# The order of weight mixing and residual rests on GpSimd in the third FFN step of a macaron block

## What is computed

```
w_eff = w * (su @ sv)                 # su, sv of rank 4
a = x @ gate_eff.T ; b = x @ up_eff.T # 512 -> 1792
d = silu(a) * b
out = d @ down_eff.T                  # 1792 -> 512
```

## Time and profile before

| | |
|---|---|
| median of 3 runs | 1234.85 us (1234.61 to 1234.9) |
| profiled execution, its own time | 1236.1 us |
| span of its instructions | 1234.8 us |
| busy: TensorE, VectorE, ScalarE, GpSimd | 1216.9, 828.5, 757.9, 652.9 us |
| mean granted TensorE clock | 0.999 |
| DMA traffic | 93.77 MB, mean 76 GB/s |

### The profile page before, as it was taken

One profiled execution on the slowest core, in us unless ns is written; L12 is line 12 of the kernel. 1 busy time (PEld: TensorE's weight loads), 2 busy tenths in 40 slices (PEclk: granted clock), 3 DMA queues, 4 the chain that ended last, 5 costly groups with the idle time before them and its releaser, 6 DMA issues.

```text
span 1234.8 us, 18595 instructions
## 1 busy us (share of the span) xinstructions
PE 1216.9 (99%) x6418; PEld 1068.0 (86%) x6418; DVE 828.5 (67%) x2002; ACT 757.9 (61%) x1762; POOL 652.9 (53%) x526
## 2 busy tenths in 40 slices
PE   6999999999999999999999999999999999999999
PEld 5888888899999999999999999999999788888887
DVE  7876665775666677677667667677677768745555
ACT  4554442357667677777767767767767764544442
POOL 4786551735675625725724724824823343865540
PEclk9999999999999999999999999999999999999999
DMA  6143232212213123122122122122122110221101
GB/s 232 43 154 110 102 104 102 95 44 86 85 36 103 45 76 103 44 78 100 38 86 95 43 86 94 44 86 87 51 86 78 26 54 16 70 68 52 52 18 68
DMA packets 33452, 93.77 MB, mean 76 GB/s; under 512 B 4112, under 2 KB 4784, under 8 KB 31312
## 3 DMA queue, kind: packets, MB, share of 16 engines
q1 hardware_dynamic: 33120, 92.29, 22.0%
q10 hardware_dynamic: 240, 0.30, 0.1%
HBM read 62.69 MB, written 29.88 MB: 75 GB/s over the span
## 4 chain that ended last, share of the span: by engine, by line
PE 92%; DVE 4%; ACT 2%; POOL 1%; issue 1%; DMA 1%; SPq 0%; DVEq 0%; ACTq 0%; POOLq 0%
PE bank L345 21%; PE bank L347 21%; PE bank L346 21%; PE bank L591 5%; PE bank L430 4%; PE bank L424 4%; PE bank L425 4%; PE bank L605 3%; PE bank L610 3%; PE bank L606 3%; PE bank L570 2%; PE bank L373 1%; DVE stats L1116 1%; PE bank L573 1%; PE bank L361 0%
## 5 line engine op out<-in xcount | busy, mean ns | idle before, releaser
L974 ACT ACTIVATE prob<-prob,neg_top 128x128 f32<-128x128 f32 (+3 forms) x256 | 141.2, 553 | 78.4 <-DVE neg_top L1386 77.8
L1665 POOL TENSOR_TENSOR rows<-rows,row_root_y 128x640 f32<-128x640 f32 x64 | 80.5, 1258 | 204.2 <-DVE row_root_y L1112 204.2
L1659 POOL TENSOR_TENSOR square<-rows 128x640 f32<-128x640 f32 x64 | 79.3, 1256 | 161.0 <-DVE rows L1422 125.1
L1534 POOL TENSOR_TENSOR w_l_late<-raw_late,w_h_late 128x512 fp32r<-128x512 f32 (+1 forms) x59 | 91.5, 1565 | 73.9 <-ACT w_h_late L728 73.9
L983 ACT ACTIVATE prob<-prob,inverse 128x128 f32<-128x128 f32 (+3 forms) x256 | 123.0, 553 | 4.4 <-DVE inverse L1391 4.4
L1397 DVE TENSOR_TENSOR probT_l<-bank,probT_h 128x512 fp32r<-128x512 f32 x160 | 101.4, 684 | 20.9 <-ACT probT_h L989 20.8
L1386 DVE CUSTOM_DVE_ANT_0 prob<-bank,bias 128x128 f32<-128x128 f32 (+3 forms) x256 | 110.0, 485 | 0.6 <-PE bank L347 0.4
L989 ACT CAST probT_h<-bank 128x512 fp32r<-128x512 f32 x160 | 84.6, 597 | 42.0 <-PE bank L591 42.0
L1178 DVE SCALAR_TENSOR_TENSOR x_rows<-bank,x_rows 128x512 f32<-128x512 f32 x112 | 75.7, 687 | 46.0 <-PE bank L430 45.9
L345 PE MATMUL bank<-o_h,oT_h 128*128 128x512 f32 x256 | 104.8, 409 | 0.0
L347 PE MATMUL bank<-o_h,oT_l 128*128 128x512 f32 x256 | 100.9, 394 | 0.0
(11 more groups left out here) (216 smaller groups left out, 3757.3 us busy)
## 6 DMA issues: line engine op xcount, KB each, us to landing
x_ring<-x_between SPq DMA_DIRECT2D x64, 256.0 KB, 2.6
x_between<-x_ring SPq DMA_DIRECT2D x56, 256.0 KB, 2.0
raw_late<-w_qkv SPq DMA_DIRECT2D x8, 1536.0 KB, 6.4
raw_early<-ffn_w SPq DMA_DIRECT2D x21, 512.0 KB, 4.1
scaled<-raw_early SPq DMA_DIRECT2D x21, 512.0 KB, 2.7
raw_late<-scaled SPq DMA_DIRECT2D x21, 512.0 KB, 3.7
raw_late<-w_o SPq DMA_DIRECT2D x8, 1024.0 KB, 5.0
x_between<-x_rows SPq DMA_DIRECT2D x8, 256.0 KB, 2.0
```

The source lines that it names most:

```text
L974: last = act.activation(p, p, ACT.Exp, bias=neg_top[:, h:h + 1], scale=-1.0, accum_out=total[:, h:h + 1])
L1534: return pool.tensor_tensor(lo, raw, hi.bitcast(F32), ALU.subtract)
```

## The change

In `ffn` GpSimd mixes the weights of step 2 before the rests of a11 and a12 of the same step, in both passes. Since the end of the mixing no longer says that the rest of a12 was made from the raw block, the load of "gu0" of step 3 waits for that rest as well, as the loads before it do.

```diff
                 if p == 0:
                     stack_ahead(2)
+
+                mix_weights(p, 2)
                 split(p, 2, "a11", "a12")
-                mix_weights(p, 2)
...
                 if kind == "gu0" and seven(p, s - 1):
                     sp.wait_ge(weights_mixed, 4 * sevens(p, s - 1))
-                if kind != "gu0" or s - 1 <= 1:
+                if kind != "gu0" or s - 1 <= 2:
                     sp.wait_ge(ffn_lo, split_nth(p, s - 1, {"gu0": "a12", "gu1": "a22", "down": "d1"}[kind]) + 1)
```

## The result

| | before | changed |
|---|---|---|
| median, six runs each | 1234.87 us (1234.61 to 1236.34) | 1246.71 us (1245.37 to 1247.05) |
| ratio, 95% interval | | 1.0088 (1.0077 to 1.0098) |
| profiled execution, its span | 1236.1, 1234.8 us | 1245.37, 1244.1 us |
| mean granted clock, profiled | 0.999 | 0.997 |

The change costs 11.8 us by the medians. The forecast was 1245.2, the range 1242.0 to 1248.0. First the page of the changed kernel, part 1; it answers to the earlier trace rows.

A forecast was written before the change was run, and what follows sets the result against it. TensorE was taken to bound the kernel, so GpSimd's lateness goes straight onto the end. 6.2 + 3.5 - 0.9 + 1.6 = 10.4 us on the median of 1234.85 gives 1245.2 us, range 1242.0 to 1248.0.

The forecast's parts named there:

- What bounds the kernel: Whole kernel: TensorE, busy 1216.9 us; other engines' lateness beyond product 1's slack in step 2 goes straight onto the end.
- Stall of pass 0, 6.2 us: TensorE at product 1 of step 2, pass 0: waits for a11's rest until 79.05, 6.2 us, bounds 4.9 to 6.8.
- the d_lo that I named at 77.35: VectorE operation in pass 0, 1.02 us, claimed not to move and to fall beside a11's rest, taken as 1.81 us.
- Stall of pass 1, 3.5 us: TensorE at product 1 of step 2, pass 1: 3.5 us, bounds 2.3 to 4.5, with mixing starting in GpSimd's 2.56 us wait.
- The stall of 0.87 us saved: TensorE's later stall at 91.19 in pass 0 goes as step 3's load gains slack: -0.9 us.
- The added wait: Step 3's first load, waiting for a12's rest: goes out 0.5 us earlier in pass 0; in pass 1 mends no stall, 0.
- The clock, 1.6 us: TensorE's clock falls to half after pass 0's stop, +1.6 us; nothing counted for pass 1 in the likeliest case.
- the row at 986: Clock fall near the end of attention in the earlier profile, 3.4 us long, 1.6 us lost; used to size the clock term.
- No fall: Rival: clock stays at 1.00 after TensorE's long stop in pass 0; 1243.7 us, chance 0.25.
- Delay made up in attention: Rival: the 3.4 us of idle time in attention shrinks and makes up some delay; 1241.8 us, chance 0.03.
- Not slower: Rival: mixing hides in GpSimd's wait for ScalarE's copy of a11, only 0.9 us saved; 1234.0 us, chance 0.02.
- Two falls, 1246.8: Rival: the clock falls after the stops of both passes, adding 1.6 us to 1245.2; chance 0.2.

The follow-up runs named there:

- pass 0 alone: Changed kernel with the mixing ahead of the rests in pass 0 only, pass 1 in the old order: 1241.89 us, ratio 1.0059.
- the filled kernel: Changed kernel plus overwritten matmuls in TensorE's stops ahead of product 1 of step 2, 24 in pass 0 and 13 in pass 1: 1243.77 us.
- the second profile: Changed kernel run once more with no edit: median 1247.31 us, ratio 1.0097; its profiled execution took 1247.88 us.

## Why the prediction was right, point by point

- **What bounds the kernel.** Right: TensorE's slack of under 0.3 us at product 1 in pass 0 and none in pass 1 was the whole matter. Moving the mixing behind a11's rest alone gave all the time back. Of what was put back and what was put ahead, TensorE in the kernel before asks for the rest of a11 at once, for that of a12 in product 2, at 81.47, and for the first mixed block in product 6:

```profile
84.22 0.39 PE L345 MATMUL bank<-mix_h,mixed_h 128*128 128x512 f32 x1
```

- **Stall of pass 0, 6.2 us.** Measured 6.03. The mixing took 5.85 for 5.96 and the rest of a11 1.68 for 1.81, and by the chain of work it ended at 78.96, for 79.0. But the d_lo that I named at 77.35 was not what it met. VectorE's timeline in the changed kernel:

```profile
71.87 3.06 DVE L1217 TENSOR_TENSOR d_lo<-d,d_hi 128x512 fp32r<-128x512 f32 x2
...
76.30 1.53 DVE L1211 TENSOR_TENSOR d<-d,silu 128x512 f32<-128x512 f32 x1 [0.17 <-ACT silu L772]
83.11 0.69 DVE L1217 TENSOR_TENSOR d_lo<-d,d_hi 128x512 fp32r<-128x512 f32 x1 [5.27 <-ACT d_hi L782]
```

  ScalarE's copy ahead of that d_lo stands behind product 1's partial sum, so it moved to 83.11, and I had said that it doesn't move. The pair of d_lo from 71.87 took 3.06 us, 1.98 before, and VectorE's product at 76.30 was the one beside the rest. The duration that I took was near, the reason given for it was not right.
- **Stall of pass 1, 3.5 us.** Measured 3.3. The mixing started right behind the down rests, as said. It was closer than I wrote. The chain that ended last, in the changed profile:

```profile
1067.82 3.58 DMA raw_late<-scaled
...
1071.55 1.28 POOL mixed L1562
...
1076.23 1.68 POOL mixed L1568
1077.90 1.23 POOL w_l_late L1534
```

  The load landed at 1071.40 and the mixing began 0.15 us later. The two durations were both off, and that they cancel is luck: the mixing took 6.4 us (1071.55 to 1077.91) for my 5.95, and the rest of a11 1.23 for my 1.75, together 7.6 for 7.7. The VectorE operation that I had meet the rest did meet it, at 1078.14, but there it was the one that took longer, 1.53 us for 0.69 at 1066.16 before.
- **The stall of 0.87 us saved.** Right in the changed kernel, 1.1 us with what hangs on it. Of the 6.7 us of slack that I gave the load, the part that counts is the late TensorE; the 0.5 us by the clock are not needed. SyncE's queue after:

```profile
80.25 7.02 SPq L1801 DMA_DIRECT2D raw_early<-ffn_w  x2
```

  Step 3's first load went out at 80.25 for 80.81. The kernel with the mixing between the rests, with its load at 80.87 and TensorE on time, kept the stall; the kernel with half of the mixing ahead, with its load at 80.94 and TensorE 3.4 us late, lost it.
- **The added wait.** Right, 0.
- **The clock, 1.6 us.** This is the term that was mis-sized. Pass 0's fall cost 2.5 us, because the half clock lasted from 77.3 to 84.1, 5.1 us of it with TensorE at work, and not for the 3.4 us of the row at 986. And there is a second fall, for which I counted nothing and gave a chance of 0.2: six of the ten runs of the changed kernel have a mean clock of 0.996, as the profile with two falls has. The one such profile has it behind pass 1's stop. In the kernel with pass 0 alone no run of four had 0.996, which speaks for that stop and against the old place near 987; more profiles would have to show it. With the measured terms 6.0 + 3.3 + 2.5 - 1.1 = 10.7 us, on the 1234.8 of the kernel before without a fall, comes 1245.5: two of the first six times lie there (1245.37, 1245.65). With 1.6 more for a second fall comes 1247.1, and the other four lie at 1246.5 to 1247.05, so the median is of that kind. Three of these four have the clock of 0.996; the slowest, 1247.05, has 0.997, as has the 1243.46 of pass 0 alone, so not every long run is explained by a second fall. The kernel before is without a fall in most runs (46 of 68 in four batches have a mean clock of 1.000). That the clock is nearly all of the remainder is shown by the filled kernel: 8.6 us without any fall, where the measured stalls give 8.2 and my terms without a fall 8.8. The forecast is 1.5 us under the median: too small by 0.9 in pass 0's fall and by the 1.6 of the second, too large by 0.4 in the two stalls, and short of what was saved by 0.2. That makes 1.9, so 0.4 us stays without a place.
- **Rivals.** No fall: out. My argument for it was a misreading: the row of the first 30 us prints 1.00, but TensorE was slow at the start of them. In the kernel before, 16 transposes of one shape take 3.27 us there and 1.91 us later in the same stretch, so that 1.00 says nothing of the clock before 14 us:

```profile
10.73 3.27 PE L373 MATMUL bank<-ident,xn 128*128 128x128 f32 x16 [2.91 <-DVE xn L1137]
...
26.90 1.91 PE L373 MATMUL bank<-ident,xn 128*128 128x128 f32 x16
```

  Delay made up in attention: out, the difference of 1.54 there is the clock of one profile. Not slower: out. Two falls, 1246.8: the nearest to the median of 1246.71, and the sum of its terms as measured, 1247.1, is within 0.4 us of it. Of the Trainium skill's rule (page "TensorE: Matmul & The Clock Gate", Part 1), that an idle TensorE is put back to half clock, the trace now shows both stops as cases, the 6.0 us one in all three profiles that have it unfilled, the 3.3 us one in one profile of three.

What stays open is what decides, in a given run, whether the fall comes behind pass 1's stop, near 987, or not at all. A series of profiles of one kernel wasn't taken.

## What to carry to other kernels

Ask of an operation moved ahead what it is moved ahead of, and how much slack the consumer of that has: here the consumer had none, and one rest needed at once went behind four operations of which the first result is needed 11 us later. On a kernel bound by TensorE a stop costs its length and can then cost the clock, as the 6.0 us one did in each of three profiles and the 3.3 us one in one of three: price both. And a saved stall should be traced to what made it, since the same 0.87 us went away with a late TensorE and with one scaling put elsewhere, but not with the earlier mixing that seemed to lead to it.

## What the runs showed of the hardware

- The clock can fall while TensorE is already at work again: in the second profile it was back at 1080.03 and the clock fell near 1081.5. In the first one the low stretch behind pass 0's stop lasted 6.8 us, twice that of the row at 986.
- The profile of the kernel before had itself lost its clock at 986 and took 1236.1 us; the runs of that kernel with a mean clock of 1.000 have medians of 1234.7 to 1234.8 by batch, those with 0.999 of 1235.9 to 1236.4. A difference of 1.4 us between two profiles of these kernels may be that alone.
- GpSimd's operations and VectorE's with two SBUF operands take longer beside each other. A pair of d_lo took 3.06 us while GpSimd was mixing without a pause (71.87 in the changed kernel) and 1.98 us where GpSimd stood idle for 0.5 us of it (before); a single d_lo beside an idle GpSimd took 0.69. GpSimd's mixing operations beside them took 1.59 and 1.71 us for 1.29.
